# A shorter search step, ranks from two scans, and expert 0's first rows in parallel pieces

## The reference

```python
N = B * S                                   # 4096 tokens
k = max(MIN_CAPACITY, ceil(N * CAPACITY_FACTOR / E))    # 1024
xt = x.reshape(N, D)
scores = jax.nn.softmax(xt @ Wr, axis=-1)
G, idx = jax.lax.top_k(scores.T, k)         # each expert's 1024 best tokens
X_in = xt[idx]
h = jax.nn.gelu(jnp.einsum('ekd,edh->ekh', X_in, W1) + b1[:, None, :], approximate=False)
X_e = jnp.einsum('ekh,ehd->ekd', h, W2) + b2[:, None, :]
contrib = (G[..., None] * X_e).reshape(E * k, D)
out = jnp.zeros((N, D), dtype=x.dtype).at[idx.reshape(-1)].add(contrib)
```

## Time and profile before

| | |
|---|---|
| median of 3 runs | 1239.88 us (1239.66 to 1241.63) |
| the profiled execution | 1239.33 us, span 1237.4 us |
| busy in the span | PE 1121.4 us (91%), DVE 830.0 (67%), ACT 692.1 (56%), POOL 819.0 (66%) |
| mean granted clock of TensorE | 0.97 |

### The profile page before, as it was taken

The page is one execution under the profiler, slowest core; times in us unless marked ns, Lnnn a source line. Parts: engine busy times, 40 slices in busy tenths (PEclk is TensorE's granted clock), DMA queues, the critical chain, the costliest instruction groups (busy, mean ns, idle before and its releaser), DMA issues. The chain is left out here.

```text
span 1237.4 us, 19984 instructions
## 1 busy us (share of the span) xinstructions
PE 1121.4 (91%) x6999; PEld 982.0 (79%) x6999; DVE 830.0 (67%) x1964; ACT 692.1 (56%) x1434; POOL 819.0 (66%) x886
## 2 busy tenths in 40 slices
PE   3899999999999999999999998117999999999997
PEld 2788888888888878878888874016999999999996
DVE  4777787887787787887887855774554555554433
ACT  3666666656656666666666654004554654655542
POOL 3797897887887888887987851014664654744534
PEclk9999999999999999999999999558999999999999
DMA  5000110110100100100100003302433523624223
GB/s 191 1 18 1 39 31 1 39 30 2 44 26 1 44 26 1 44 27 3 46 22 35 18 1 108 107 13 57 121 81 67 129 38 101 134 35 108 26 26 34
DMA packets 42211, 58.09 MB, mean 47 GB/s; under 512 B 8897, under 2 KB 34945, under 8 KB 41985
## 3 DMA queue, kind: packets, MB, share of 16 engines
q0 software_dynamic: 13824, 21.24, 9.8%
q1 hardware_dynamic: 28288, 35.58, 8.7%
HBM read 35.71 MB, written 16.91 MB: 43 GB/s over the span
## 5 line engine op out<-in xcount | busy, mean ns | idle before, releaser
L1098 DVE TENSOR_TENSOR hT_lo<-hid,hT_hi 128x512 fp32r<-128x512 f32 x124 | 86.4, 697 | 170.1 <-ACT hT_hi L1245 157.2
L198 POOL TENSOR_SCALAR prob<-prob,row_inv 128x512 f32<-128x512 f32 (+3 forms) x256 | 135.3, 541 | 69.1 <-DVE row_inv L418 67.4
L1242 ACT ACTIVATE hid<-up,b_e 128x512 f32<-128x512 f32 x128 | 88.1, 688 | 150.4 <-PE up L1345 136.1
L272 ACT ACTIVATE prob<-prob,row_min 128x512 f32<-128x512 f32 (+3 forms) x256 | 142.4, 556 | 40.1 <-DVE row_min L411 39.3
L867 POOL DMA_INDIRECT x<-routed_rows,tokens x64 | 84.3, 1318 | 112.7 <-DVE tokens L1092 95.0
L354 DVE TENSOR_TENSOR pT_lo<-bank,pT_hi 128x384 fp32r<-128x384 f32 (+1 forms) x192 | 114.3, 595 | 42.4 <-ACT pT_hi L254 42.4
L878 POOL TENSOR_SCALAR y<-y,gate 128x256 f32<-128x256 f32 x60 | 32.4, 552 | 128.0 <-issue 127.2
L411 DVE CUSTOM_DVE_ANT_0 prob<-bank,mask_row 128x512 f32<-128x512 f32 (+3 forms) x256 | 114.1, 483 | 0.0
L206 POOL TENSOR_TENSOR q_sin<-q_sin,rope_t 128x512 f32<-128x512 f32 x64 | 82.5, 1290 | 43.6 <-ACT q_sin L296 42.0
L887 POOL DMA_INDIRECT out<-y,tokens x60 | 97.2, 1621 | 16.1 <-issue 13.9
L600 PE MATMUL bank<-ident,prob 128*128 128x128 f32 x640 | 101.7, 273 | 5.6 <-POOL prob L198 5.6
(11 more groups left out here) (239 smaller groups left out, 3821.7 us busy)
## 6 DMA issues: line engine op xcount, KB each, us to landing
raw<-in_w SPq DMA_DIRECT2D x16, 1024.0 KB
emb_res<-emb SPq DMA_DIRECT2D x8, 512.0 KB, 3.7
out<-h SPq DMA_DIRECT2D x8, 512.0 KB, 2.9
routed_rows<-x SPq DMA_DIRECT2D x8, 512.0 KB, 3.1
x<-in_wq SPq DMA_DIRECT2D x1, 1024.0 KB, 5.1
x<-in_wk SPq DMA_DIRECT2D x1, 1024.0 KB, 4.9
x<-in_wv SPq DMA_DIRECT2D x1, 1024.0 KB, 7.0
x<-in_wo SPq DMA_DIRECT2D x1, 1024.0 KB, 10.1
```

Of the source, the lines that this page charges most:

```text
L198: nc.gpsimd.tensor_scalar(pr, pr, row_inv[:, h % 2, k:k + 1], 1.0, ALU.mult, ALU.mult).then_inc(s["norm_done"], 1)
L272: nc.scalar.activation(pr, pr, ACT.Exp, bias=row_min[:, h % 2, k:k + 1], scale=-1.0, accum_out=row_sum[:, h % 2, k:k + 1]).then_inc(s["exp ...
L1098: nc.vector.tensor_tensor(out, in_, hi.bitcast(F32), ALU.subtract)\
L1242: nc.scalar.activation(hid[:, t % 2, :], up_ps[t % 2][:], ACT.Gelu, bias=bias)
```

## The change

Five things, all in `build_middle`:

1. The search keeps the next three candidates themselves. While TensorE sums, VectorE adds a constant (`back`) to the old candidates (`base3`), and one fused instruction makes the new ones from `steps` and `base3`. That holds for the upper bits (iterations 0 to 10, `FUSED` = 11); below, lower and upper bits are kept apart (`low_cand`, `high`) and joined by an or, one instruction more. The first candidates are constants.
2. The ranks come from two scans that start from zero and need no sum over partitions first; the sums over partitions (four small products) are added at the end in `need`.
3. Expert 0's places are made first, those of the other seven after its one-hot tiles. For expert 0 the token part of `hot_b` is made by ScalarE, which has first run one small Gelu.
4. Expert 0's first two turned chunks go to two banks (`x_ps` and `up_ps[1]`), and the first `up` unit waits for the second chunk only in its middle.
5. Expert 0 has the list of expert 2 at t = 4 in place of t = 2.

```diff
+        first_x_ps = [x_ps, up_ps[1]]
...
+            for k in range(3):
+                nc.gpsimd.memset(cand[:, k:k + 1], (k + 1) << 28).then_inc(s["c_const"], 1)
+                for z in range(2):
+                    nc.gpsimd.memset(step_bits[:, z, k:k + 1], (k + 1) << (4 - 2 * z))\
                         .then_inc(s["c_const"], 1)
+                for r in range(ITERATIONS):
+                    nc.gpsimd.memset(back[:, r, k:k + 1],
+                                     -(k + 1) << (28 - 2 * r) if r in (FUSED, ITERATIONS - 1)
+                                     else -3 * (k + 1) << (26 - 2 * r)).then_inc(s["c_const"], 1)
...
-                dve.wait_ge(s["s_step"], 4 * r + 1)
-                nc.vector.tensor_tensor(cand[:], step_bits[:, r, :], least[:].to_broadcast([P, 3]),
-                                        ALU.bitwise_or).then_inc(s["s_step"], 1)
-                dve.wait_ge(s["s_step"], 4 * r + 2)
...
+                if r < FUSED:
+                    search_step(nc.vector.tensor_tensor(base3[:], cand[:], back[:, r, :], ALU.add))
+                elif r != FUSED + 1:
+                    before = cand if r == FUSED else low_cand
+                    search_step(nc.vector.tensor_tensor(base3[:], before[:], back[:, r, :], ALU.add))
...
+                search_step(nc.vector.tensor_scalar(enough[:], l_ps[:, 0:3], float(TOPK), None,
+                                                    ALU.is_ge, ALU.add, accum_out=steps[:]))
+                dve.wait_ge(s["s_step"], at[0])
+                if r < FUSED:
+                    search_step(nc.vector.scalar_tensor_tensor(cand[:], thrice, delta, base3[:],
+                                                               ALU.mult, ALU.add))
+                elif r == FUSED:
+                    search_step(nc.vector.scalar_tensor_tensor(high[:], steps[:], delta, base3[:, 0:1],
+                                                               ALU.mult, ALU.add))
+                    dve.wait_ge(s["s_step"], at[0])
+                    search_step(nc.vector.tensor_tensor(cand[:], step_bits[:, 0, :],
+                                                        high[:].to_broadcast([P, 3]), ALU.bitwise_or))
...
+                    rest = step_bits[:, 1, :] if r == FUSED + 1 else base3[:]
+                    search_step(nc.vector.scalar_tensor_tensor(low_cand[:], thrice, delta, rest,
+                                                               ALU.mult, ALU.add))
+                    dve.wait_ge(s["s_step"], at[0])
+                    search_step(nc.vector.tensor_tensor(cand[:], low_cand[:],
+                                                        high[:].to_broadcast([P, 3]), ALU.bitwise_or))
...
-                nc.vector.tensor_scalar(steps_i[:], steps[:], float(1 << (28 - 2 * r)), None, ALU.mult)\
-                    .then_inc(s["s_step"], 1)
...
+            mark(above, ALU.is_gt, 0)
+            mark(equal, ALU.is_equal, 1).then_inc(s["counted"], 1)
+            dve.wait_ge(s["counted"], ITERATIONS + 1)
+            prefix(before_a, above)
+            chained(prefix(before_e, equal))
+            nc.vector.scalar_tensor_tensor(before_a, above, -4.0 * TOPK, before_a, ALU.mult, ALU.add)
+            dve.wait_ge(s["ranked"], 1)
+            chained(nc.vector.tensor_scalar(need[:], l_ps[:, 4:6], -1.0, float(TOPK),
                                             ALU.mult, ALU.add))
-            mark(equal, ALU.is_equal).then_inc(s["marked"], 1)
-            ranks(equal, 1)
-            chained(nc.vector.scalar_tensor_tensor(chosen, flat_rank, need[:, 0:1], equal,
-                                                   ALU.is_le, ALU.mult))
-            chained(nc.vector.tensor_tensor(chosen, chosen, above, ALU.add))
-            with nc.allow_low_precision(reason="counts up to 256 are exact in bfloat16"):
-                nc.vector.tensor_reduce(count_bf[:, 0:1], chosen, AX.X, ALU.add)\
-                    .then_inc(s["marked"], 1)
-            ranks(chosen, 2)
-
-            nc.vector.scalar_tensor_tensor(flat_rank, chosen, -4.0 * TOPK, flat_rank,
-                                           ALU.mult, ALU.add).then_inc(s["marked"], 1)
+            nc.vector.scalar_tensor_tensor(chosen, before_e, need[:, 0:1], equal, ALU.is_le, ALU.mult)
+            chained(nc.vector.tensor_scalar(before_e, before_e, need[:, 0:1], need[:, 1:2],
+                                            ALU.min, ALU.subtract))
+            chained(nc.vector.scalar_tensor_tensor(before_a, chosen, -4.0 * TOPK, before_a,
+                                                   ALU.mult, ALU.add))
+            nc.vector.tensor_tensor(rank[:].rearrange("p c t -> p (c t)"), before_a, before_e, ALU.add)\
+                .then_inc(s["marked"], 1)
...
+            def places(e0, e1):
+
+                chained(nc.vector.tensor_scalar(
+                    place[:, e0:e1, :].rearrange("p e (b c) -> p c e b", c=2),
+                    x_ps[:, 0:E * NB].rearrange("p (c e b) -> p c e b", c=2, e=E)[:, :, e0:e1, :],
+                    5.0 * TOPK - 1.0, None, ALU.add))
+                nc.vector.tensor_scalar(place_a[:, e0:e1, :], place[:, e0:e1, :], 5, None,
+                                        ALU.logical_shift_right)
+                chained(nc.vector.tensor_scalar(place_b[:, e0:e1, :], place[:, e0:e1, :], LIST_A - 1,
+                                                None, ALU.bitwise_and))
+                nc.vector.tensor_copy(at_b[:, e0:e1, :], place_b[:, e0:e1, :])
+                nc.vector.tensor_copy(at_a[:, e0:e1, :], place_a[:, e0:e1, :])\
+                    .then_inc(s["placed"], 1)
             dve.wait_ge(s["turned"], 2)
-            chained(nc.vector.tensor_scalar(place[:].rearrange("p e (b c) -> p c e b", c=2),
-                                            x_ps[:, 0:E * NB].rearrange("p (c e b) -> p c e b", c=2, e=E),
-                                            4.0 * TOPK - 1.0, None, ALU.add))
-            chained(nc.vector.tensor_scalar(place_a[:], place[:], 5, None, ALU.logical_shift_right))
-            chained(nc.vector.tensor_scalar(place_b[:], place[:], LIST_A - 1, None, ALU.bitwise_and))
-            nc.vector.tensor_copy(at_a[:], place_a[:])
-            chained(nc.vector.tensor_copy(at_b[:], place_b[:]))
+            places(0, 1)
...
+                if e > 0:
+                    nc.vector.tensor_tensor(hot_a[:], spread(at_a, e), wide_iota, ALU.is_equal)
+                nc.vector.tensor_tensor(hot_b[:, :, 0, :], spread(at_b, e), wide_iota, ALU.is_equal)\
                     .then_inc(s["l_chain"], 1)
+                if e == 0:
+                    nc.vector.tensor_tensor(hot_a[:], spread(at_a, e), wide_iota, ALU.is_equal)
                 dve.wait_ge(s["l_chain"], e * 3 + (chain0 + 1))
-                nc.vector.tensor_scalar(hot_b[:, :, 1, :], hot_b[:, :, 0, :], tok_no[:, 0:1], None,
-                                        ALU.mult)
+                if e > 0:
+                    nc.vector.tensor_scalar(hot_b[:, :, 1, :], hot_b[:, :, 0, :], tok_no[:, 0:1], None,
+                                            ALU.mult)
                 nc.vector.tensor_tensor(hot_b[:, :, 2, :], hot_b[:, :, 0, :],
                                         blk_no[:].unsqueeze(2).to_broadcast([P, NB, LIST_A]),
...
+                src = first_x_ps[kt] if e == 0 and g == 0 else x_ps
+                low(xT[i][1][:, kt, cols], src[:], xT[i][0][:, kt, cols], "e_xt_lo")
...
             one_hots(0)
+            places(1, E)
             write_list(0, 0)
             first_bias(0, 0)
+            dve.wait_ge(s["placed"], 2)
             one_hots(1)
...
+            act.wait_ge(s["r_const"], 1)
+            nc.scalar.activation(gelu_first[:], neg_half[:, 0:1], ACT.Gelu)
+            act.wait_ge(s["l_chain"], 1)
+            nc.scalar.activation(hot_b[:, :, 1, :], hot_b[:, :, 0, :], ACT.Copy, scale=tok_no[:, 0:1])\
+                .then_inc(s["hot_b0"], 1)
...
+            for k, terms in enumerate([((0, 0), (1, 1)), ((1, 0), (1, 1))]):
+                for n, (which, col) in enumerate(terms):
+                    last = nc.tensor.matmul(l_ps[:, 4 + k:5 + k], groups[:, which, :],
+                                            count_bf[:, col:col + 1], start=n == 0, stop=n == 1)
+            last.then_inc(s["ranked"], 1)
+            pe.wait_ge(s["marked"], 1)
...
-                after(pe, "e_xt_lo", 4 * e + f)
+                first = e == 0 and g == 0
+                if not first:
+                    after(pe, "e_xt_lo", 4 * e + f)
+                out = first_x_ps[kt] if first else x_ps
...
+                    if t == 0 and c == len(PARTS):
+                        after(pe, "e_xt_lo", 4 * e + 2)
...
+            pe.wait_ge(s["hot_b0"], 1)
...
-                        after(pe, "e_xt_lo", 4 * e + 2)
+                        after(pe, "e_xt_lo", 4 * e + 1)
...
-                    if more2 and t == 2:
+                    if more2 and t == (4 if e == 0 else 2):
```

80 lines of the change are left out of this document (38 added, 42 removed).

## The result

The changed kernel took 1232.38 us (median of 4 runs, 1230.02 to 1233.12) beside 1239.91 for the kernel before: 0.9933 of it, 95% interval 0.9916 to 0.9950. The forecast of 1227.3 with a range of 1224.5 to 1231.0 missed it by 5.1 us. What lies between those numbers is the subject of this part.

The account below looks back on a forecast made before the run. The expert phase was taken as bound by TensorE and only shifted by a shorter serial chain before it. Savings summed to 12.5 us: 1239.33 to 1226.8, plus 0.55 for the median, 1227.3 us, range 1224.5 to 1231.0.

Parts of the forecast that it names:

- Search, ranks, places, one-hot: Serial chain before the first gather: shorter instruction chains were to save 5.0, 1.14, 0.92 and 0.51 us.
- Rival B: In the search, the added integer sum is not hidden, costing 2.7 us, so 1230.0 us; chance 12%.
- First rows: Before the first up products: the second chunk, turned into a second bank, no longer waits; 2.50 us saved.
- Table and moved list: First units: ScalarE's table loaded during the search saves 1.30 us, the third list's products two steps later 1.15.
- The clock: First units: granted clock rises 3.0 us after the first up product; earlier gains 1.3 us, later loses 0.8.
- Rival C: Second list or first units: a signal comes later still, losing 0.4 to 2 us, about 1228.8; chance 11%.
- Sum: All savings together: 12.5 us off the profiled 1239.33 gives 1226.8; with the median 0.55 above, 1227.3 us.

Follow-up runs that it names:

- the paced kernel: Changed kernel with the gathers of experts 1 and 2 issued one per up unit; 1227.79, 1227.41 and 1226.95 us in three groups of runs.
- g1_same: Changed kernel run again without an edit, on another chip; 1227.12 us, 0.9900 of the kernel before.
- h1_same: Changed kernel run once more without an edit, on a further chip; 1226.33 us, 0.9890 of the kernel before.
- c1_same: Changed kernel run again without an edit, beside other follow-up runs on one chip; 1232.11 us, 0.9946 of the kernel before.
- e3_list_t2: Changed kernel with the third list's products moved back behind the first down unit (t = 2); 1234.40 us, 0.9947 of the kernel before.

## Why the prediction missed, by its own steps

- **Search, ranks, places, one-hot** (7.57 us: 5.0 + 1.14 + 0.92 + 0.51). From the score's turning products to the first gather it was 52.82 us and is 45.12 (821.65 - 776.53): 7.70. By parts: search 4.93 (0.20 ahead of the first comparison, 33.01 to 28.28 from there to the fifteenth), ranks 1.30 (5.85 to 4.55), places 0.82, one-hot 0.43; 0.20 more came from the scores' turning products themselves, which ended sooner and for which no term stood. Rival B falls: the integer sum is 0.16 us and hidden.
- **First rows** (2.50). B went from 12.33 to between 9.75 and 9.80: 2.5 to 2.6. Right.
- **Table and moved list** (1.30 + 1.15 = 2.45). C is 2.6 us shorter in every trace without holds of the unedited and the paced kernel, 1.20 of it from the table and 0.94 from the list; for the other 0.4 to 0.5 there is no run. TensorE waited 0.00 to 0.30 us at the second down unit (g1_same none, h1_same 0.19, first profile 0.30), where I had 0.4.
- **The clock.** It rose 3.5 us after the first up product in the first profile and 3.8 to 4.4 in the two unedited ones without holds (h1_same: 831.34 to 835.13; g1_same: 832.73 to 837.15), not 3.0. That is within the range given.
- **Rival C, the late signal**, is the step that failed: the sum puts late signals at nothing, and takes each wait of the first units as ending with the product that it waits for. The rival was named, from the earlier trace rows, with 11% and "0.4 to 2 us", worked out as one delay of 1.5 us that grows or falls on a tighter wait. Measured: TensorE's signals held one behind the other by up to 6.0 us, 3.73 us of idle time, and a fall of the clock for 6.82 us; C 5.2 to 6.5 us longer (c1_same, first profile) than without. The trace of before held two more such signals, 2.0 and 2.1 us late at 849.43 and 850.86, just where the change moves products up against GpSimd's gathers. I read the one row and not the list of signals.
- **Sum.** On the two chips without holds the unedited kernel is 0.9900 (0.9884 to 0.9917) and 0.9890 (0.9873 to 0.9907), 1227.12 and 1226.33 us: the forecast of 1227.3 was right for these, by its own terms (A 7.3, B 2.6 and C 2.6 us shorter), and wrong by 5.1 us for the result and by 4.8 for c1_same. Which kind of execution the result would be was chance as far as the prediction goes: nothing in it tells the two apart.

What stays open is why signals are held in some groups of runs and not in others, and whether it is the chip or the time that decides. That records are lost in the same traces points to the path that carries records, and it would fit that TensorE pauses inside a unit (e3_list_t2) and that it takes a row of issues before holding starts. It was only argued: every execution here was recorded, so none shows whether an unrecorded one is held too. The Trainium skill ("NOTIFIC — the notification-queue block", Overflow: three behaviours, one of which stalls the engine) describes that block as pressing back on its producers when its inner queues fill, rather than losing a record there, with a counter for it, which no run here read. Late signals and pauses would fit that; the missing records would need another cause beside it.
